# Local attention with half-summed products: additions on GpSimd and VectorE ahead of TensorE's sums, a tree for VectorE's own sums, and a last block shared anew

## The chip, the cores and the metric

One core of a Trainium2 chip runs the whole program. The metric is the device time of one execution in microseconds (us), taken over several runs. The engines are TensorE (PE), VectorE (DVE), ScalarE (ACT), GpSimd (POOL) and SyncE (SP); SBUF is the on-chip memory of 128 partitions, PSUM the memory into which TensorE accumulates.

## The reference

Four layers run one after the other on x of 8 x 512 x 256: a causal attention, a transformer layer with four experts, the local attention `_L0_attn_b_ref`, and the transformer layer once more. Each is `x = x + layer(layernorm(x))`. The change touches the local attention alone:

```python
def _L0_attn_b_ref(query, in_proj_weight, in_proj_bias, rel_pos_keys, out_w, out_b):
    t, b, e = query.shape
    scaling = D ** (-0.5)
    qkv = jnp.einsum('tbe,fe->tbf', query, in_proj_weight) + in_proj_bias
    q, k, v = jnp.split(qkv, 3, axis=-1)
    ...
    scores = jnp.einsum('btd,bsd->bts', q, k) + jnp.einsum('btd,tsd->bts', q, rel_k)
    probs = jax.nn.softmax(scores, axis=-1)
    attn = jnp.einsum('bts,bsd->btd', probs, v)
    attn = attn.transpose(1, 0, 2).reshape(t, b, e)
    return jnp.einsum('tbe,oe->tbo', attn, out_w) + out_b
```

Its first axis is the "time": x is given as it is, so there are 8 times, and 512 sequences take the place of the batch. Each of 16 heads has 16 elements. A query attends to all 8 times of its own sequence, so scores are 8 x 8 per sequence and head: far too small for matmuls over a sequence.

## The kernel before, in words

`local_attention` puts 128 sequences on the partitions and goes through four blocks (`bt`, NBT = 4). In a block, t is the time of the query and s that of the key, both 0 to 7. All is 32-bit.

For each t and block, two kinds of product of 128 x 2048 (8 keys x 256 elements) are made elementwise:
- score products, query t times all keys, which VectorE reduces over the 16 elements of a head into `s_ps` (PSUM), line 2207;
- value products, the weights of t times all values, which are then summed over the 8 keys s.

Who makes them: GpSimd makes the score products of t = 0 to 5 (`scores`, line 2362) and the value products of t = 0, 1, 2, 4, 5 (`values`, line 2370) into a ring of four buffers; VectorE makes the score products of 6 and 7 (line 2193, the query read from `a_ps` in PSUM) and the value products of 3, 6 and 7 (`own_values`, line 2243, the weights read from `s_ps` in PSUM) into `own[0]` and `own[1]`.

Who sums the value products over the keys: TensorE for t = 0 to 5 (`sum_over_keys`, line 1997), with eight matmuls by the identity that accumulate 256 columns each in one half of `att_ps`; two values of t fill it, and the next pair waits until VectorE's `normalise` (line 2263) has read it. For 6 and 7 VectorE's own reduce does it (line 2248).

Around that: TensorE projects block bt + 1 (lines 1952 to 1977) and the output of block bt - 1 (lines 2009 to 2019) while block bt's scores and weights are made, and then runs block bt's sums; in the last block there is nothing left to project ahead. ScalarE reads the projections out of PSUM and takes the exponentials (lines 2107 and 2111). VectorE adds the relative term, subtracts the maximum (`shift`), totals the weights (`total_weight`, lines 2229 and 2231), normalises and adds the residual (`add_residual`, line 2269). The order on each engine is written out by hand, and all is tied by counting semaphores, so every engine works strictly in its own written order. The transformer phases before and after are blocks of their own and don't overlap with these four.

Of the kernel before, what the change touches and what calls it, by code (L numbers as in the profile page):

```python
# [1811 lines left out]
NTM = NB  # L1812
# [9 lines left out]
N_POOL = len(POOL_QK) + len(POOL_PV)  # L1822
N_DVE = len(DVE_QK) + len(DVE_PV)
# [3 lines left out]
def local_attention(nc, ctx, C, A, x_src, x_dst):  # L1827
# [59 lines left out]
    def qk_order(t):  # L1887

        return t - DVE_QK[0] if t in DVE_QK else len(DVE_QK) + t

    def pool_item(bt, t, pv):
        return N_POOL * bt + (len(POOL_QK) + POOL_PV.index(t) if pv else POOL_QK.index(t))

    def dve_item(bt, t, pv):
        return N_DVE * bt + (len(DVE_QK) + DVE_PV.index(t) if pv else DVE_QK.index(t))

    with nc.Block() as block:
# [25 lines left out]
        def _(pe):  # L1923
# [31 lines left out]
            def project_qk(bt, t):  # L1955
# [75 lines left out]
            for bt in range(NBT):  # L2031
# [21 lines left out]
                for t in PE_SUMS:  # L2053
# [6 lines left out]
        def _(act):  # L2060
# [40 lines left out]
            def exp(bt, q):  # L2101
                act.wait_ge(shifted, 2 * bt + q + 1)
                if bt >= 1:
                    act.wait_ge(pool_prod, N_POOL * bt)
# [3 lines left out]
                first = 3 if q == 0 else 2  # L2108
# [335 lines left out]
```

## Time and profile before

| | us |
|---|---|
| median of 3 runs (2695.67 to 2700.51) | 2695.88 |
| the profiled execution | 2708.65 |
| its span, first to last instruction | 2706.9 |
| the four blocks of the local attention in it | 275.1 |
| TensorE busy over the span | 2469.7 (91%) |
| VectorE | 1834.3 (68%) |
| ScalarE | 1437.0 (53%) |
| GpSimd | 1344.7 (50%) |

These shares are means over phases with different limits. The four blocks are a tenth of the span, and what a change in them is worth is read from their own stretch: the view by windows for busy time, and the timelines of the engines for what each waits for. In a timeline a row is one instruction or several alike, merged (x32); the brackets give the idle time before it and what ended it.

### The profile page before, as it was taken

To read this page: it belongs to the slowest core of one execution; us is meant where nothing else is said; L and a number is where in the kernel's file an instruction comes from. 1 tells how busy PE (TensorE), PEld (TensorE's weight loads), DVE (VectorE), ACT (ScalarE), POOL (GpSimd) and SP (SyncE) were. 2 spreads that over 40 slices of the span, in tenths; PEclk is the share of its full clock that TensorE was granted. 3 is DMA by queue.
4 is the path that set the end of the run, shared out by engine and by line. 5 is a ranking of instruction groups with operands and counts; after the bars stand their busy time and mean duration, and the time that the engine had idled before them with its cause. 6 is when DMAs were issued, how large, how long until landed. Compare 5 with 4: busy or idle time off the path is not lost. (4 is left out here: it accounts for less than half of the span.)

```text
span 2706.9 us, 46628 instructions
## 1 busy us (share of the span) xinstructions
PE 2469.7 (91%) x15144; PEld 1428.9 (53%) x15144; DVE 1834.3 (68%) x3670; ACT 1437.0 (53%) x2991; POOL 1344.7 (50%) x1359
## 2 busy tenths in 40 slices
PE   4999999999999999989994899976999999989997
PEld 2455555554444444368894466652344444349896
DVE  3899999998778887833333566755778888844333
ACT  2666666666777777643331222102777777653332
POOL 4466555653345554246453466633335555445554
PEclk8999999999999999999997799986999999999998
DMA  5333333333434444146554000004334444335553
GB/s 149 88 107 106 99 97 106 114 114 91 120 119 130 131 125 115 48 145 195 185 194 146 0 1 16 16 31 123 107 113 129 131 130 123 91 113 176 188 200 115
DMA packets 250018, 306.35 MB, mean 113 GB/s; under 512 B 27692, under 2 KB 224945, under 8 KB 249780
## 3 DMA queue, kind: packets, MB, share of 16 engines
q1 hardware_dynamic: 239604, 277.11, 34.2%
q0 software_dynamic: 10176, 26.27, 2.7%
q8 instruction: 125, 2.05, 0.3%
q14 instruction: 113, 0.93, 0.1%
HBM read 210.85 MB, written 92.84 MB: 112 GB/s over the span
## 5 line engine op out<-in xcount | busy, mean ns | idle before, releaser
L698 DVE TENSOR_REDUCE neg_max_af<-sc_af 128x1 f32<-128x512 f32 (+3 forms) x864 | 550.8, 664 | 122.0 <-PE sc_af L414 86.2
L628 ACT ACTIVATE prob_af<-sct_af 128x512 f32<-128x512 f32 (+1 forms) x864 | 484.9, 582 | 253.7 <-PE sct_af L435 139.8
L698 DVE TENSOR_REDUCE neg_max_f<-sc_f 128x1 f32<-128x512 f32 x512 | 334.3, 685 | 102.7 <-PE sc_f L414 100.0
L628 ACT ACTIVATE prob_f<-sct_f 128x512 f32<-128x512 f32 x512 | 291.4, 598 | 143.0 <-PE sct_f L435 140.4
L414 PE MATMUL sc_af<-stack_k_af,stack_q_af 96*128 96x512 bf16 (+3 forms) x1024 | 333.0, 345 | 15.5 <-DVE neg_max_af L698 15.1
L435 PE MATMUL sct_af<-stack_q_af,stack_k_af 99*128 99x512 bf16 (+3 forms) x1024 | 331.2, 345 | 6.8 <-ACT prob_af L628 5.4
L1513 PE MATMUL hT_ps_e<-xT_e,w_r 128*128 128x128 f32 x2240 | 266.6, 278 | 5.1 <-DMA w_r<-in_f_W_dram 4.0
L1513 PEld LDWEIGHTS hT_ps_e<-xT_e,w_r 128*128 128x128 f32 x2240 | 264.4, 194 | 10.7 <-DMA w_r<-in_f_W_dram 6.0
L1500 PE MATMUL y_ps_e<-w_r,hT_e 128*128 x1120 | 256.5, 382 | 5.9 <-issue 3.8
L727 DVE SCALAR_TENSOR_TENSOR prob_af<-prob_af,w_r 128x512 f32<-128x512 f32 (+2 forms) x224 | 234.3, 1054 | 25.4 <-ACT prob_af L628 25.3
L466 PE MATMUL out_af<-prob_af,v_aug_af 128*32 128x512 f32 (+3 forms) x2048 | 231.8, 524 | 7.2 <-DVE prob_af L727 6.3
L1500 PEld LDWEIGHTS y_ps_e<-w_r,hT_e 128*128 128x128 f32 x1120 | 208.2, 191 | 35.8 <-issue 9.9
L435 PEld LDWEIGHTS sct_af<-stack_q_af,stack_k_af 99*128 99x128 bf16 x1024 | 100.0, 98 | 229.7 <-ACT prob_af L628 148.6
L1665 DVE TENSOR_TENSOR y_e<-y_ps_e,b_e 128x256 f32<-128x256 f32 x70 | 29.7, 425 | 282.3 <-PE y_ps_e L1500 278.1
L414 PE MATMUL sc_f<-stack_k_f,stack_q_f 96*128 96x512 bf16 x512 | 198.8, 390 | 9.5 <-DVE neg_max_f L698 9.5
L435 PE MATMUL sct_f<-stack_q_f,stack_k_f 99*128 99x512 bf16 x512 | 195.1, 383 | 5.9 <-ACT prob_f L628 4.4
L1550 ACT ACTIVATE xT_e<-xT_ps_e 128x256 f32<-128x256 f32 x70 | 26.9, 384 | 324.5 <-PE xT_ps_e L1491 303.5
L1561 ACT ACTIVATE hT_e<-hT_ps_e,b_r 128x128 f32<-128x128 f32 x560 | 152.8, 383 | 32.9 <-issue 26.9
L414 PEld LDWEIGHTS sc_af<-stack_k_af,stack_q_af 96*128 96x128 bf16 x1024 | 101.6, 99 | 125.3 <-DVE neg_max_af L698 61.4
L966 POOL TENSOR_TENSOR parts_af<-qkf_af,parts_af 128x512 bf16<-128x512 f32 x64 | 80.6, 1259 | 148.3 <-ACT parts_af L606 148.3
L466 PE MATMUL out_f<-prob_f,v_aug_f 128*32 128x512 f32 x1024 | 136.4, 604 | 0.8 <-ACT prob_f L628 0.7
L435 PEld LDWEIGHTS sct_f<-stack_q_f,stack_k_f 99*128 99x128 bf16 x512 | 49.6, 98 | 160.1 <-ACT prob_f L628 119.2
(358 smaller groups left out, 4658.3 us busy)
## 6 DMA issues: line engine op xcount, KB each, us to landing
w_r<-in_f_W_dram SPq DMA_DIRECT2D x78, 1024.0 KB, 6.3
k_parts_d<-parts_af SPq DMA_DIRECT2D x192, 128.0 KB
stack_k_af<-k_parts_d SPq DMA_DIRECT2D x64, 384.0 KB, 4.3
q_parts_d<-parts_af SPq DMA_DIRECT2D x96, 128.0 KB
stack_q_af<-q_parts_d SPq DMA_DIRECT2D x64, 192.0 KB, 3.0
k_parts_d<-parts_f SPq DMA_DIRECT2D x96, 128.0 KB
stack_k_f<-k_parts_d SPq DMA_DIRECT2D x32, 384.0 KB, 4.3
xt_r<-sorted_x SPq DMA_DIRECT2D x70, 128.5 KB
```

The lines of the kernel that those rows point to most:

```text
L414: last = nc.tensor.matmul(bank[:, o:o + cols], M.stack_q[0:96, g, h, qt * P:qt * P + P], M.stack_k[0:96, g, h, 0:cols], start=True, stop=True)
L435: last = nc.tensor.matmul(bank[:, o:o + T - q0], M.stack_k[0:99, g, h, kt * P:kt * P + P], M.stack_q[0:99, g, h, q0:T], start=True, stop=True)
L466: last = nc.tensor.matmul(bank[32 * i:32 * i + 32, q0:T], M.v_aug[:, kt, 4 * g + i, :], M.prob[:, kt % 2, i, 0:T - q0], start=(kt == 0), s ...
L628: nc.scalar.activation(dst, src.rearrange("p (h q) -> p h q", h=len(heads)), ACT.Exp).then_inc(S.exp_done, 1)
L698: nc.vector.tensor_reduce(M.neg_max[:, qt, heads[0]:heads[-1] + 1], src, AX.X, ALU.max, negate=True).then_inc(S.max_done, 1)
L727: nc.vector.scalar_tensor_tensor(out=p, in0=p, scalar=1.0, in1=M.floor[:, g % 2, hs, kt * P:T], op0=ALU.min, op1=ALU.max).then_inc(S.clip_ ...
L966: nc.gpsimd.tensor_tensor(M.parts[:, j, 1, :], full, top, ALU.subtract).then_inc(S.split_step, 1)
L1500: last = nc.tensor.matmul(y_ps[:, 0:D], hT[s % 2][:, c, :], w2[:, c, e, :], start=(c == 0), stop=(c == FC - 1))
L1513: last = nc.tensor.matmul(hT_ps[2 * (s % 2) + f][:, q * P:q * P + P], w1[n % NW][:, c, cols], xT[:, c, :], start=(c == 0), stop=(c == DC - 1))
L1550: nc.scalar.activation(xT[:, :, :], xT_ps[:, 0:D].rearrange("p (c t) -> p c t", c=DC), ACT.Copy).then_inc(xT_ready, 1)
L1561: last = nc.scalar.activation(hT[s % 2][:, 4 * f + q, :], hT_ps[2 * (s % 2) + f][:, q * P:q * P + P], ACT.Relu, bias=b1[:, e, 4 * f + q:4 ...
L1665: nc.vector.tensor_tensor(y[i][:, :], y_ps[:, 0:D], b2[:, e, :], ALU.add).then_inc(y_ready, 1)
```

## The change

- In blocks 0 to 2 GpSimd adds the two halves of the value products of t = 1, 2 and 5 onto each other (1024 columns), waiting for its own product first, and TensorE's sum for these takes four matmuls.
- `own_values` adds its product's halves with `fold` (1024 columns, then 512), waits between the steps, and for t = 3 leaves two slices to TensorE; for 6 and 7 a third addition of 256 columns ends in `att`. The reduce of line 2248 is gone.
- The last block is shared anew: GpSimd makes the score products of 0 to 4 and the value products of 0 to 3, VectorE the score products of 6, 7 and 5 (5 with the query from `qk` in SBUF) and the value products of 4 to 7; TensorE sums in the order 0, 1, 4, 2, 5, 3, with 4 and 5 in `b_ps` and two slices each. VectorE's order for that block is written out by itself.

```diff
-POOL_QK = (0, 1, 2, 3, 4, 5)
-DVE_QK = (6, 7)
-POOL_PV = (0, 1, 2, 4, 5)
-DVE_PV = (3, 6, 7)
-PE_SUMS = (0, 1, 2, 3, 4, 5)
+LAST = NBT - 1
+POOL_QK = [(0, 1, 2, 3, 4) if bt == LAST else (0, 1, 2, 3, 4, 5) for bt in range(NBT)]
+DVE_QK = [(6, 7, 5) if bt == LAST else (6, 7) for bt in range(NBT)]
+POOL_PV = [(0, 1, 2, 3) if bt == LAST else (0, 1, 2, 4, 5) for bt in range(NBT)]
+DVE_PV = [(4, 5, 6, 7) if bt == LAST else (3, 6, 7) for bt in range(NBT)]
+PRE_ADDED = [() if bt == LAST else (1, 2, 5) for bt in range(NBT)]
+PE_SUMS = [(0, 1, 4, 2, 5, 3) if bt == LAST else (0, 1, 2, 3, 4, 5) for bt in range(NBT)]
...
-    def qk_order(t):
-
-        return t - DVE_QK[0] if t in DVE_QK else len(DVE_QK) + t
+    def qk_order(bt, t):
+
+        order = [6, 7] + [u for u in range(8) if u < 6] if bt < LAST else [6, 0, 7, 1, 5, 2, 3, 4]
+        return order.index(t)
...
+    def summands(bt, t):
+
+        if t in PRE_ADDED[bt]:
+            return NTM // 2
+        return 2 if t in DVE_PV[bt] else NTM
+
+    def own_buf(bt, t):
+
+        if bt == LAST and t in DVE_PV[bt]:
+            return own[(4, 5, 6, 7).index(t) % 2]
+        return own[0] if t == 3 else own[1]
...
-                if t in POOL_PV:
+                if t in POOL_PV[bt]:
                     m = pool_item(bt, t, True)
                     pe.wait_ge(pool_prod, m + 1)
                     buf = ring[m % RING]
                 else:
-                    pe.wait_ge(dve_prod, dve_item(bt, t, True) + 1)
-                    buf = own[0]
+                    pe.wait_ge(own_added, added_by_vector(bt, t))
+                    buf = own_buf(bt, t)
                 n = 3 * bt + t // 2
-                if t % 2 == 0 and n >= 1:
+                sums = b_ps if bt == LAST and t >= 4 else att_ps
+                if bt == LAST and t >= 4:
+                    pe.wait_ge(b_read, NTM * NBT)
+                elif t % 2 == 0 and n >= 1:
                     pe.wait_ge(normed, 4 * ((n - 1) // 3) + (n - 1) % 3 + 1)
-                for s in range(NTM):
-                    last = nc.tensor.matmul(att_ps[:, D * (t % 2):D * (t % 2) + D], C.ident[:, :], buf[:, s * D:s * D + D],
-                                            start=(s == 0), stop=(s == NTM - 1))
+                for s in range(summands(bt, t)):
+                    last = nc.tensor.matmul(sums[:, D * (t % 2):D * (t % 2) + D], C.ident[:, :], buf[:, s * D:s * D + D],
+                                            start=(s == 0), stop=(s == summands(bt, t) - 1))
                 last.then_inc(pe_summed, 1)
...
-                first = 3 if q == 0 else 2
+                first = (3 if q == 0 else 2) if bt < LAST else (3 if q == 0 else 0)
...
+            def fold(dst, buf, cols):
+
+                folds[0] += 1
+                nc.vector.tensor_tensor(dst, buf[:, 0:cols], buf[:, cols:2 * cols], ALU.add).then_inc(fold_step, 1)
+                dve.wait_ge(fold_step, folds[0])
...
+                if t == 5:
+                    dve.wait_ge(qk_summed, NTM * bt + qk_order(bt, 7) + 1)
...
-                q = a_ps[t % 2][:, 0:D].rearrange("p (h e) -> p h e", h=H).unsqueeze(1).to_broadcast(wide)
+                q = (qk[i][:, t, 0:D] if t == 5 else a_ps[t % 2][:, 0:D]).rearrange("p (h e) -> p h e", h=H).unsqueeze(1).to_broadcast(wide)
                 nc.vector.tensor_tensor(split_heads(own[t % 2]), k, q, ALU.mult).then_inc(dve_prod, 1)
...
-                buf = own[0] if t == 3 else own[1]
+                buf = own_buf(bt, t)
                 dve.wait_ge(weights_ready, 4 * bt + (2 if t < 4 else 4))
-                if t == 3:
+                if bt < LAST and t == 3:
                     dve.wait_ge(qk_summed, NTM * bt + 2)
-                if t == 7:
+                if bt == LAST and t in (4, 5):
+                    dve.wait_ge(qk_summed, NTM * bt + NTM)
+                if bt == LAST and t in (6, 7):
+                    dve.wait_ge(pe_summed, N_SUMS * bt + PE_SUMS[bt].index(t - 2) + 1)
+                if bt < LAST and t == 7:
                     dve.wait_ge(own_summed, 2 * bt + 1)
                 v = vr[i][:, :, 0:D].rearrange("p s (h e) -> p s h e", h=H)
                 wt = s_ps[t // 4][:, (t % 4) * P:(t % 4) * P + P].rearrange("p (s h) -> p s h", s=NTM).unsqueeze(3).to_broadcast(wide)
                 nc.vector.tensor_tensor(split_heads(buf), v, wt, ALU.mult).then_inc(dve_prod, 1)
-                if t != 3:
-                    dve.wait_ge(dve_prod, dve_item(bt, t, True) + 1)
+                dve.wait_ge(dve_prod, dve_item(bt, t, True) + 1)
+                fold(buf[:, 0:4 * D], buf, 4 * D)
+                if t < 6:
+                    nc.vector.tensor_tensor(buf[:, 0:2 * D], buf[:, 0:2 * D], buf[:, 2 * D:4 * D], ALU.add).then_inc(own_added, 1)
+                else:
+                    fold(buf[:, 0:2 * D], buf, 2 * D)
                     if bt >= 1 and t == 6:
                         dve.wait_ge(oT_made, 4 * bt)
-                    nc.vector.tensor_reduce(att[:, t, :], buf[:, :].rearrange("p (s c) -> p c s", s=NTM), AX.X, ALU.add).then_inc(own_summed, 1)
+                    nc.vector.tensor_tensor(att[:, t, :], buf[:, 0:D], buf[:, D:2 * D], ALU.add).then_inc(own_summed, 1)
...
                 if j < 3:
-                    dve.wait_ge(pe_summed, len(PE_SUMS) * bt + 2 * j + 2)
+                    dve.wait_ge(pe_summed, N_SUMS * bt + max(PE_SUMS[bt].index(t) for t in (2 * j, 2 * j + 1)) + 1)
...
-                    src = att_ps[:, :].rearrange("p (t h e) -> p t h e", t=2, h=H)
+                    src = (b_ps if bt == LAST and j == 2 else att_ps)[:, :].rearrange("p (t h e) -> p t h e", t=2, h=H)
...
+            own_scores(LAST, 6)
+            pool_scores(LAST, 0)
+            own_scores(LAST, 7)
+            pool_scores(LAST, 1)
+            own_products(LAST, 5)
+            own_scores(LAST, 5)
+            add_residual(LAST - 1, 0)
+            pool_scores(LAST, 2)
+            pool_scores(LAST, 3)
+            shift(LAST, 0)
+            add_residual(LAST - 1, 1)
+            pool_scores(LAST, 4)
+            shift(LAST, 1)
+            total_weight(LAST, 0)
+            own_values(LAST, 4)
+            own_values(LAST, 5)
+            total_weight(LAST, 1)
+            normalise(LAST, 0)
+            own_values(LAST, 6)
+            normalise(LAST, 1)
+            own_values(LAST, 7)
+            normalise(LAST, 2)
+            normalise(LAST, 3)
...
-                nc.gpsimd.tensor_tensor(split_heads(ring[m % RING]), v, weight[:, t, :, :].unsqueeze(3).to_broadcast(wide),
-                                        ALU.mult).then_inc(pool_prod, 1)
+                buf = ring[m % RING]
+                made = nc.gpsimd.tensor_tensor(split_heads(buf), v, weight[:, t, :, :].unsqueeze(3).to_broadcast(wide), ALU.mult)
+                if t in PRE_ADDED[bt]:
+                    made.then_inc(pool_step, 1)
+                    pool.wait_ge(pool_step, len(PRE_ADDED[0]) * bt + PRE_ADDED[bt].index(t) + 1)
+                    made = nc.gpsimd.tensor_tensor(buf[:, 0:4 * D], buf[:, 0:4 * D], buf[:, 4 * D:8 * D], ALU.add)
+                made.then_inc(pool_prod, 1)
```

## Rows read from the trace of the kernel before

**Rows 1.** Windows view, the four blocks; per engine busy us (instructions), then PEclk, DMA.
```profile
1547.10:1607.20 60.10, 57.47 (x235) 36.90 (x234) 31.53 (x21) 16.37 (x33) 30.51 (x8) 1.00 0.00 1
1607.20:1678.80 71.60, 69.40 (x289) 44.65 (x288) 49.03 (x33) 18.05 (x36) 45.74 (x12) 1.00 0.05 15
1678.80:1750.50 71.70, 69.50 (x289) 44.67 (x288) 49.02 (x33) 14.13 (x28) 45.86 (x12) 1.00 0.05 15
1750.50:1822.20 71.70, 54.38 (x209) 38.73 (x207) 47.90 (x37) 6.38 (x12) 33.50 (x9) 0.86 0.04 15
```

**Rows 2.** Timeline of TensorE, block 1: start us, length us, engine, line, operation.
```profile
1655.78 7.07 PE L1997 MATMUL att_ps_l<-ring_l,ident 128*128 128x256 f32 x32
1663.79 3.69 PE L1997 MATMUL att_ps_l<-ring_l,ident 128*128 128x256 f32 x16 [0.93 <-DVE att_l L2263]
...
1671.86 7.14 PE L1997 MATMUL att_ps_l<-ring_l,ident 128*128 128x256 f32 x32 [0.93 <-DVE att_l L2263]
1678.84 1.04 PE L1952 MATMUL g_ps_l<-ident,xn_l 128*128 128x128 f32 x8
```

**Rows 3.** Timeline of GpSimd in the four blocks.
```profile
1572.54 14.61 POOL L2370 TENSOR_TENSOR ring_l<-vr_l,weight_l 128x2048 f32<-128x2048 f32 x4 [28.94 <-ACT weight_l L2107]
...
1644.23 14.61 POOL L2370 TENSOR_TENSOR ring_l<-vr_l,weight_l 128x2048 f32<-128x2048 f32 x4 [17.68 <-ACT weight_l L2107]
...
1663.12 9.03 POOL L2362 TENSOR_TENSOR ring_l<-qk_l 128x2048 f32<-128x2048 f32 x2
...
1769.73 18.24 POOL L2370 TENSOR_TENSOR ring_l<-vr_l,weight_l 128x2048 f32<-128x2048 f32 x5 [1.68 <-ACT weight_l L2107]
```

**Rows 4.** Timeline of VectorE, block 1.
```profile
1649.95 2.28 DVE L2243 TENSOR_TENSOR own_l<-vr_l,s_ps_l 128x2048 f32<-128x2048 f32 x1
1652.69 1.02 DVE L2229 TENSOR_REDUCE total_l<-weight_l 128x64 f32<-128x512 f32 x1 [0.47 <-ACT weight_l L2107]
...
1656.48 3.77 DVE L2248 TENSOR_REDUCE att_l<-own_l 128x256 f32<-128x2048 f32 x1
1662.95 0.69 DVE L2263 TENSOR_TENSOR att_l<-att_ps_l,inv_l 128x512 f32<-128x512 f32 x1 [2.69 <-PE att_ps_l L1997]
...
1671.03 0.69 DVE L2263 TENSOR_TENSOR att_l<-att_ps_l,inv_l 128x512 f32<-128x512 f32 x1 [1.41 <-PE att_ps_l L1997]
```

**Rows 5.** Timeline of GpSimd in the first layer.
```profile
321.20 0.74 POOL L983 TENSOR_TENSOR v_aug_af<-v_st_af,ones 128x256 f32<-128x256 f32 x1 [5.19 <-ACT v_st_af L573]
...
353.80 1.18 POOL L970 TENSOR_TENSOR parts_af<-qkf_af,parts_af 128x512 bf16<-128x512 f32 x1
355.98 1.76 POOL L983 TENSOR_TENSOR v_aug_af<-v_st_af,ones 128x256 f32<-128x256 f32 x1 [1.01 <-PE out_af L474]
357.82 1.32 POOL L990 TENSOR_TENSOR w_r<-v_aug_af 128x128 f32<-128x128 f32 x1
```

**Rows 6.** Timeline of VectorE in the same stretch.
```profile
353.99 1.02 DVE L711 TENSOR_TENSOR max_rest_af<-neg_max_af,max_parts_af 128x16 f32<-128x16 f32 x1
...
355.94 2.88 DVE L727 SCALAR_TENSOR_TENSOR prob_af<-prob_af,w_r 128x1024 f32<-128x1024 f32 x2
```

**Rows 7.** Views of single lines: count, ns min/median/max, first and last start.
```profile
L2263 DVE TENSOR_TENSOR att_l<-att_l,inv_l x4: 681/990/1002, 1608.1 to 1808.1; 128x512 f32<-128x512 f32 x4
...
L2362 POOL TENSOR_TENSOR ring_l<-qk_l x24: 4507/4532/4988, 1516.7 to 1763.5; 128x2048 f32<-128x2048 f32 x24
```

**Rows 8.** Groups by shape: count | busy us, mean ns | idle before.
```profile
L711 DVE TENSOR_TENSOR max_rest_f<-neg_max_f,max_parts_f 128x16 f32<-128x16 f32 x32 | 5.7, 179 | 1.1
...
L1602 DVE TENSOR_TENSOR x_out_r<-x_out_r,ln_b 128x1024 f32<-128x1024 f32 x2 | 2.4, 1224 | 0.1
...
L1044 POOL TENSOR_TENSOR x_out_r<-x_out_r,ln_g 128x1024 f32<-128x1024 f32 x14 | 30.6, 2186 | 0.0
```

**Rows 9.** Timeline of TensorE, block 3.
```profile
1790.05 5.84 PE L1997 MATMUL att_ps_l<-ring_l,ident 128*128 128x256 f32 x16 [7.72 <-DVE att_l L2263]
```

**Rows 10.** Windows view, 2 us at that sum's start.
```profile
1790.00:1792.00 2.00, 1.95 (x5) 1.62 (x6) 2.00 (x1) 0.00 (x0) 0.00 (x0) 0.50 0.00 0
```

More of the change, by code:

```diff
@@ L1816 @@
 NB_COLS = 3 * D + NREL * H
-POOL_QK = (0, 1, 2, 3, 4, 5)
-DVE_QK = (6, 7)
-POOL_PV = (0, 1, 2, 4, 5)
-DVE_PV = (3, 6, 7)
-PE_SUMS = (0, 1, 2, 3, 4, 5)
-N_POOL = len(POOL_QK) + len(POOL_PV)
-N_DVE = len(DVE_QK) + len(DVE_PV)
+LAST = NBT - 1
[5 more added lines that the diff above has]
+PE_SUMS = [(0, 1, 4, 2, 5, 3) if bt == LAST else (0, 1, 2, 3, 4, 5) for bt in range(NBT)]
+N_SUMS = 6
+N_POOL = [len(POOL_QK[bt]) + len(POOL_PV[bt]) for bt in range(NBT)]
+N_DVE = [len(DVE_QK[bt]) + len(DVE_PV[bt]) for bt in range(NBT)]
 RING = 4
@@ L2052, in _ @@
                         project_out(bt - 1, q)
-                for t in PE_SUMS:
+                for t in PE_SUMS[bt]:
                     sum_over_keys(bt, t)
@@ L2079, in free_inputs @@
                 if bt >= 2:
-                    act.wait_ge(pool_prod, N_POOL * (bt - 1))
-                    act.wait_ge(dve_prod, N_DVE * (bt - 1))
+                    act.wait_ge(pool_prod, sum(N_POOL[:bt - 1]))
+                    act.wait_ge(dve_prod, sum(N_DVE[:bt - 1]))
             def read_qk(bt, t):
@@ L2103, in exp @@
                 if bt >= 1:
-                    act.wait_ge(pool_prod, N_POOL * bt)
+                    act.wait_ge(pool_prod, sum(N_POOL[:bt]))
                     act.wait_ge(inv_step, 4 * bt)
@@ L2215, in shift @@
                 base = 2 * (2 * bt + q)
-                dve.wait_ge(qk_summed, NTM * bt + max(qk_order(t) for t in range(4 * q, 4 * q + 4)) + 1)
+                dve.wait_ge(qk_summed, NTM * bt + max(qk_order(bt, t) for t in range(4 * q, 4 * q + 4)) + 1)
                 dve.wait_ge(b_read, NTM * bt + NTM)
@@ L2293, in _ @@
             shift_of(1, NBT - 1)
-            for t in DVE_QK:
+            for t in (6, 7):
                 own_products(0, t)
-            for bt in range(NBT):
-                for t in DVE_QK:
+            for bt in range(NBT - 1):
+                for t in (6, 7):
                     own_scores(bt, t)
@@ L2317, in _ @@
                 normalise(bt, 1)
-                if bt + 1 < NBT:
-                    for t in DVE_QK:
-                        own_products(bt + 1, t)
+                for t in (6, 7):
+                    own_products(bt + 1, t)
                 normalise(bt, 2)
                 normalise(bt, 3)
+            own_scores(LAST, 6)
[21 more added lines that the diff above has]
+            normalise(LAST, 3)
             add_residual(NBT - 1, 0)
@@ L2349, in free_ring @@
                     return
[L2350 to L2352 removed]
+                old_bt, at = 0, m - RING
+                while at >= N_POOL[old_bt]:
+                    old_bt, at = old_bt + 1, at - N_POOL[old_bt]
+                if at < len(POOL_QK[old_bt]):
+                    pool.wait_ge(qk_summed, NTM * old_bt + qk_order(old_bt, POOL_QK[old_bt][at]) + 1)
                 else:
[L2354 removed]
+                    pool.wait_ge(pe_summed, N_SUMS * old_bt + PE_SUMS[old_bt].index(POOL_PV[old_bt][at - len(POOL_QK[old_bt])]) + 1)
             def scores(bt, t):
@@ L2375, in _ @@
             for bt in range(NBT):
-                for t in POOL_QK:
+                for t in POOL_QK[bt]:
                     scores(bt, t)
-                for t in POOL_PV:
+                for t in POOL_PV[bt]:
                     values(bt, t)
```

18 lines of the change are left out of this document (9 added, 9 removed).

## The prediction, made before the changed kernel ran

> **What bounds the kernel now.** I looked first for the stretch in which the changed function runs, with the view by windows: four blocks, 1547.1 to 1822.2 us, 275.1 of the span's 2706.9 [rows 1]. Nothing outside it is touched, and the phases on both sides are separated from it, so only these four lengths can move. In blocks 0 to 2 TensorE (PE) is busy 57.5 of 60.1, 69.4 of 71.6 and 69.5 of 71.7 us at a granted clock of 1.00: it is the bound. In block 3 it is busy 54.4 of 71.7 and the clock's mean is 0.86: there it waits for other engines.
>
> Second, TensorE's own order in block 1, which block 2 repeats to 0.02 us [rows 2]. After the next block's projections come six sums over keys; two sums take 7.07 us, so one sum of eight matmuls takes 3.54 and one matmul 0.44. Between pairs it idles only 0.93 us, for VectorE's normalisation. Third, what stands beside it. GpSimd (POOL) starts its value products at 1644.23, right behind the exponentials, and makes one every 3.65 us; a score product takes 4.52 [rows 3]. VectorE's (DVE) order behind the exponentials is product 3 (2.28 us), the weights' total with its reciprocal (1652.69 to product 6, which ends at 1656.48: 1.55), product 6 and its reduce (3.77), normalise 0 at 1662.95, product 7 and reduce, normalise 1 at 1671.03 [rows 4]. So both helpers are done just in time: normalise 0 and 1 wait for TensorE, not the other way round.
>
> **What the change removes.** In blocks 0 to 2 sums 1, 2 and 5 shrink from eight matmuls to four, sum 3 from eight to two: 18 of 48, or 18 x 0.44 = 7.9 us of TensorE per block. Two reduces of 3.77 us go too.
>
> **What it adds, uncontended.** VectorE gets eight additions: for buffer 3 two (1024 and 512 columns), for 6 and 7 three each (1024, 512, 256). A 1024-column addition takes 1.22 us [rows 8]; a 512-column product 0.68 at its shortest [rows 7]; the 256-column one I estimate at 0.42 from their difference. A tree is then 2.3 us where the reduce took 3.77, and buffer 3 costs 1.9 more. GpSimd gets three 1024-column instructions at 2.19 us [rows 8], 6.6 us per block; they stand in its queue ahead of the later products. Their waits on the instruction before cost some 0.1 us each, an estimate from GpSimd's gaps (355.98 + 1.76 to 357.82, 0.08 us) [rows 5].
>
> Laid out from 1644.23 with these alone: VectorE ends product 3 at 1652.2, its additions 1654.1, total 1655.6, product 6 at 1657.9, tree 1660.2. TensorE ends sums 0 and 1 at 1655.8 + 5.3 = 1661.1; normalise 0 to 1661.8; sums 2 and 3 to 1664.5; product 7 and tree to 1666.4, normalise 1 to 1667.0, sums 4 and 5 to 1672.4. GpSimd would have product 5 ready at 1644.2 + 18.2 + 6.8 = 1669.2, in time for that. The block would end at 1672.4, not 1678.84: 6.4 us shorter.
>
> **The term that turns it: additions with both inputs in SBUF.** Until now VectorE's large products in these blocks read one input from PSUM (the query in a_ps, the weights in s_ps), and they take 2.23 to 2.28 us whatever GpSimd does [rows 4]. All eight new additions read both inputs from SBUF. Where such instructions of VectorE meet GpSimd's, the trace shows exclusion by whole instructions, both ways:
> - A 128x16 subtraction, 0.18 us elsewhere [rows 8], starts at 353.99, 0.19 us into a GpSimd instruction that ends at 354.98, and takes 1.02: it ends at 355.01 [rows 5, 6].
> - At 355.94 two 1024-column instructions of VectorE take 2.88 us instead of 2 x 1.22. GpSimd's 355.98, whose like takes 0.74 alone, takes 1.76, so it began some 1.0 later, when the first was through; the second began when that ended [rows 5, 6]. They alternate, although VectorE's two stand back to back.
> - In this stretch: normalise 3, the only such instruction here, has a median of 0.99 us and a minimum of 0.68, and a score product has a maximum of 4.99 beside a median of 4.53 [rows 7].
> The waits end 0.13 us ahead of the recorded end of the other. I take this as the rule for the long products too. The nearest rows reach only 0.4 us into a long one, so this is the unknown; its lower bound is no wait at all (the layout above), its upper a full 3.65 or 4.52 us for each addition.
>
> The Trainium skill has the same in "SBUF — State Buffer", § Who interferes with whom: a VectorE instruction with two SBUF inputs contends with a GpSimd instruction that reads SBUF, and the shared pair of ports is held for a whole instruction while the other blocks fully. By that rule, the trace agrees (1.02 us for 0.18), the saving above is not to be had; by a sharing of bandwidth it mostly would.
>
> **Block 1 laid out again, with alternation.** GpSimd: product 0 to 1647.9, product 1 to 1651.5, its addition to 1653.8. VectorE: product 3 to 1652.2, then its 1024-addition waits to 1653.7 and ends 1654.9. GpSimd's product 2, held up, runs to 1658.4; VectorE's 512-addition waits for it, ends 1658.95. Total to 1660.5, product 6 to 1662.75. GpSimd: addition of 2 to 1661.0, product 4 to 1664.65. VectorE's tree for 6: 1664.5 to 1665.75; GpSimd's product 5 to 1669.25; VectorE 512 to 1669.75; GpSimd's addition of 5 to 1671.8; VectorE 256 to 1672.1. Normalise 0 ends 1672.75, where it ended at 1663.6. Product 7 to 1675.0; its tree waits for the next block's score products 0 and 1 (to 1676.4 and 1681.9) and ends 1682.9, the last addition free since GpSimd then waits for a ring buffer. Normalise 1 ends 1683.5, for 1671.7. TensorE, long done with sums 2 and 3, starts sum 4 at 1683.6: 5.3 us for sums 4 and 5 at full clock, end 1688.9, 10.1 later than 1678.84.
>
> The clock adds to that. TensorE now stands still for some 12 us before sum 2 and some 6 before sum 4. In block 3 of the trace it stood still 7.72 us before 1790.05, and the sum there took 5.84 us for 3.54: the granted clock was 0.50, the lower level of 1.2 GHz, when it began [rows 9, 10]. Those 2.3 us I take for sum 4; nothing and 3.5 (the whole sum at half the clock) are the bounds. The block then ends at 1691.2, **12.4 us longer**.
>
> Block 0 has the same distance from GpSimd's first value product to its end (1572.54 to 1607.2, 34.7 us, for 34.6 in block 1) [rows 1, 3] and block 2 repeats block 1, so the same for each: 3 x 12.4 = 37.2.
>
> **Block 3.** It is shared anew: GpSimd makes 5 + 4 products for 6 + 5, VectorE 3 + 4 for 2 + 3, with four trees in all, and TensorE adds 36 slices for 48 (5.3 us less). But GpSimd enters it late, with three score products left, the third waiting 2.3 us behind VectorE's product 5 (both inputs in SBUF). That product and its sum stand ahead of the residual additions, which TensorE's second output projection waits for. Laid out in the same way, an estimate with coarser steps, GpSimd has its first value product 25.5 us into the block for 19.2 [rows 3], the last ends at 40 for 37.5, and TensorE has its last sum at 58.2 for 56.9. Behind that, product 7 with its tree (4.6 us) stands between normalise 1 and the residual, while TensorE projects: the tail is 15.6 for 14.9. Sum +2; between -2 (TensorE's saving gets through at the clock's upper level) and +6.
>
> **Sum.** 37.2 + 2 = 39.2 us. The profiled execution would take 2708.65 + 39 = 2748; it lies 12.8 above the median of the timed runs, so the median goes from 2695.88 to **2735 us**. Low: 3 x 10.1 - 1.5 = 28.8, so 2725; high: 3 x 15 + 5 = 50, so 2746. With a little for the phases of the alternation, 2721 to 2751.
>
> **The rivals.**
> 1. *No wait, or a short one, behind long products* (the other side). The port is held only for a part of a 3.65 or 4.52 us instruction, so VectorE's additions slip in. For it: the only rows in a long product reach 0.4 us into its end. Against it: a 1.18 us GpSimd instruction held VectorE for all that was left. Price: 3 x -6.4 - 1.4 = -20.6, so 2675; with 0.3 us per addition and 0.45 per 512 columns on GpSimd [rows 7] some 2.3 per block remain: 2689. It decides where the median wait of a 1024-addition is under some 0.8 us. Chance 0.09.
> 2. *The tree goes through as a group.* VectorE keeps the port for all three additions, so each tree waits once. Then tree 6 ends at 1663.4, tree 7 at 1669.1, and GpSimd's last addition at 1674.9 sets the end: 1676.7, 2.1 shorter. 3 x -2.1 + 1 = -5.3: 2691. Against it: 2.88 and the 1.76 between. Chance 0.06.
> 3. *The forecast without the clock's fall*: 3 x 10.1 + 2 = 32: 2728. It is inside the range.
> That the change doesn't shorten TensorE's sums is excluded: it issues fewer matmuls of the same shape.
>
> **Chances.** Forecast with rival 3: 0.85; rivals 1 and 2: 0.09 and 0.06. The range holds nearly all of the first, some 0.81. A difference of 0.2% (5.4 us) is about what timing this kernel can tell from none. Faster by more: 0.09 and half of rival 2, 0.12; within: 0.03; slower: 0.85.
>
> **What would show it.** In the profile after: VectorE's 1024- and 512-column additions in the local attention with medians of 2.5 to 4.5 us and not 1.22 and 0.68, with the shortest ones near the latter, in block 3 after GpSimd's last product; VectorE's products with a PSUM input still at 2.26; GpSimd's products over 3.65 by up to 1.1 where an addition went ahead; TensorE idle some 12 us before sum 2 in the name of VectorE's normalise, and some 6 before sum 4; blocks of 73, 84, 84 and 74 us. Additions of 1.2 to 1.6 us beside a busy GpSimd would make the prediction wrong, and blocks of 54, 65 and 65 us would be their result. If the additions wait but normalise 0 isn't late, the layout is wrong. If sum 4 takes 3.5 us, the clock term is.

## The result, and the profile after

The changed kernel takes 2742.28 us (median of 4 runs, 2736.83 to 2745.46) where the kernel before takes 2696.74 (4 runs, 2695.67 to 2700.51): ratio 1.0164, 95% interval 1.0142 to 1.0186. It is slower by 45.5 us; 2735 was forecast, with 2721 to 2751 as the range.

In what follows, product t, sum t and tree t are those of the query time t (a tree is VectorE's chain of additions of 1024, 512 and 256 columns for t = 6 or 7), and normalise j is the instruction for t = 2j and 2j + 1.

Time first, by the four blocks. The view by windows of the profile after (per engine, PE, PEld, DVE, ACT, POOL: busy us and instructions; then the granted clock), to be read against [rows 1]:

```profile
1535.70:1609.30 73.60, 54.14 (x199) 33.23 (x197) 48.22 (x27) 16.37 (x33) 40.01 (x12) 0.86 0.00 0
1609.30:1694.60 85.30, 66.27 (x254) 41.09 (x253) 67.39 (x39) 18.05 (x36) 56.54 (x15) 0.88 0.04 13
1694.60:1779.90 85.30, 66.31 (x253) 41.08 (x252) 67.41 (x39) 14.12 (x28) 56.50 (x15) 0.88 0.04 13
1779.90:1853.50 73.60, 47.46 (x185) 32.82 (x183) 58.21 (x47) 6.60 (x12) 28.14 (x7) 0.81 0.04 15
```

The last block ends at 1854.05, so the four take 318.3 us for 275.1, 43.2 more. TensorE issues 36 records fewer in block 0 and is busy 3.3 us less, and yet the first three blocks are each 13.5 to 13.7 us longer: it waits, and the mean granted clock falls from 1.00 to 0.86 and 0.88. The profiled execution took 2739.55 us, only 30.9 more than the one of before; the parts outside the blocks, which the change doesn't touch, were 12.3 us shorter in it. So the block lengths are compared here, not the spans.

TensorE in block 1 (timeline: start, length, line; in brackets the idle time before and what ended it), against [rows 2]:

```profile
1657.90 5.35 PE L2021 MATMUL att_ps_l<-ring_l,ident 128*128 128x256 f32 x24
1675.53 3.55 PE L2021 MATMUL att_ps_l<-ring_l,ident 128*128 128x256 f32 x8 [12.28 <-DVE att_l L2305]
1678.92 1.03 PE L2021 MATMUL att_ps_l<-own_l,ident 128*128 128x256 f32 x4
1686.35 8.40 PE L2021 MATMUL att_ps_l<-ring_l,ident 128*128 128x256 f32 x24 [6.41 <-DVE att_l L2305]
1694.60 1.04 PE L1973 MATMUL g_ps_l<-ident,xn_l 128*128 128x128 f32 x8
```

The two idle times were 0.93 each in [rows 2]; they are 12.28 and 6.41, both ended by VectorE's normalisation (line 2305). The x24 of the first pair of sums takes 5.35 us and the x24 of the last pair 8.40, which is the clock; the window at its start:

```profile
1686.00:1688.00 2.00, 1.65 (x4) 1.41 (x5) 2.00 (x2) 0.00 (x0) 0.00 (x0) 0.50 0.04 8
```

GpSimd in block 1, against [rows 3] (line 2437 makes the value products, 2441 is the new addition, 2428 makes the next block's score products):

```profile
1646.35 7.32 POOL L2437 TENSOR_TENSOR ring_l<-vr_l,weight_l 128x2048 f32<-128x2048 f32 x2 [17.68 <-ACT weight_l L2131]
1653.75 2.35 POOL L2441 TENSOR_TENSOR ring_l<-ring_l 128x1024 f32<-128x1024 f32 x1
1656.06 4.67 POOL L2437 TENSOR_TENSOR ring_l<-vr_l,weight_l 128x2048 f32<-128x2048 f32 x1
1660.80 2.70 POOL L2441 TENSOR_TENSOR ring_l<-ring_l 128x1024 f32<-128x1024 f32 x1
1663.47 8.29 POOL L2437 TENSOR_TENSOR ring_l<-vr_l,weight_l 128x2048 f32<-128x2048 f32 x2
...
1674.46 10.13 POOL L2428 TENSOR_TENSOR ring_l<-qk_l 128x2048 f32<-128x2048 f32 x2
```

VectorE beside it, against [rows 4] (2281 product, 2213 and 2285 additions, 2290 the last of a tree):

```profile
1652.08 2.28 DVE L2281 TENSOR_TENSOR own_l<-vr_l,s_ps_l 128x2048 f32<-128x2048 f32 x1
1654.39 2.79 DVE L2213 TENSOR_TENSOR own_l<-own_l 128x1024 f32<-128x1024 f32 x1
1657.22 4.06 DVE L2285 TENSOR_TENSOR own_l<-own_l 128x512 f32<-128x512 f32 x1
...
1662.73 2.23 DVE L2281 TENSOR_TENSOR own_l<-vr_l,s_ps_l 128x2048 f32<-128x2048 f32 x1
1664.99 7.31 DVE L2213 TENSOR_TENSOR own_l<-own_l 128x1024 f32<-128x1024 f32 x2
1672.34 2.45 DVE L2290 TENSOR_TENSOR att_l<-own_l 128x256 f32<-128x256 f32 x1
1674.71 0.68 DVE L2305 TENSOR_TENSOR att_l<-att_ps_l,inv_l 128x512 f32<-128x512 f32 x1
...
1677.61 7.54 DVE L2213 TENSOR_TENSOR own_l<-own_l 128x1024 f32<-128x1024 f32 x2
1685.18 0.43 DVE L2290 TENSOR_TENSOR att_l<-own_l 128x256 f32<-128x256 f32 x1
```

Read the two lists together. VectorE's addition of 1654.39 ends at 1657.18, 1.1 us after GpSimd's addition (to 1656.10); GpSimd's product of 1656.06 takes 4.67 for 3.65, since it stood behind VectorE's; the 512-column addition waits that product out and ends at 1661.28, GpSimd's addition of 1660.80 takes 2.70 for 2.35. Here they alternate. Tree 6 is 9.8 us long (1664.99 to 1674.79) where the reduce took 3.77, and normalise 0 stands behind it; tree 7 meets the score products in the same way. The products of line 2281, with the weights in PSUM, are at 2.23 and 2.28 as before.

In block 3, once GpSimd has made its last product, the same instructions on VectorE:

```profile
1823.96 1.23 DVE L2213 TENSOR_TENSOR own_l<-own_l 128x1024 f32<-128x1024 f32 x1
1825.22 0.69 DVE L2285 TENSOR_TENSOR own_l<-own_l 128x512 f32<-128x512 f32 x1
...
1830.18 1.95 DVE L2213 TENSOR_TENSOR own_l<-own_l 128x1024 f32<-128x1024 f32 x2
1832.17 0.43 DVE L2290 TENSOR_TENSOR att_l<-own_l 128x256 f32<-128x256 f32 x1
```

1.23, 0.69 and 0.43 us, a tree in 2.4. Over the four blocks, by shape (count, busy us, mean ns, idle before):

```profile
L2213 DVE TENSOR_TENSOR own_l<-own_l 128x1024 f32<-128x1024 f32 x13 | 30.9, 2376 | 0.4
...
L2213 DVE TENSOR_TENSOR own_l<-own_l 128x512 f32<-128x512 f32 x8 | 28.1, 3516 | 0.3
```

A 512-column addition costs more than a 1024-column one: the length is the wait, not the work.

### The profile page after: what moved, and what is told of

It reads as the page before. It is cut to its first block and busy times, and to the rows that moved or that the text cites. A ratio compares the mean times of both kernels' runs of the same rounds, so it can differ in the third digit from the quotient of the medians.

```text
span 2737.8 us, 46402 instructions
## 1 busy us (share of the span) xinstructions
PE 2447.1 (89%) x15012; PEld 1409.5 (51%) x15012; DVE 1895.7 (69%) x3698; ACT 1436.7 (52%) x2991; POOL 1367.5 (50%) x1366
## 5 line engine op out<-in xcount | busy, mean ns | idle before, releaser
L635 ACT ACTIVATE w_r<-sct_af,minus 128x512 f32<-128x512 f32 x128 | 87.6, 687 | 86.5 <-PE sct_af L449 85.1
```

The costliest lines, as they stand in the source:

```text
L635: nc.scalar.activation(M.floor[:, g % 2, i, :], M.sct[u % 2][:, :], ACT.Exp, bias=C.minus100[:, 0:1]).then_inc(S.exp_done, 1)
```

## The experiments

Theory: VectorE's additions with both inputs in SBUF and GpSimd's instructions exclude each other as wholes, and that wait, on the way to normalise 0 and 1, with the clock's fall behind it, is the whole loss in blocks 0 to 2. Rival: the loss is work that was put on the helpers (three GpSimd additions per block, two instructions for one reduce) or the new last block. Three kernels do one part alone and a fourth two of them; they come from one source with three switches. The lengths of the blocks of all kernels are in a table at the end of this section. (The ratios and intervals are those of the recorded comparisons with the kernel before; the quotients of the two medians differ from them by up to 0.0013.)

```diff
+LASTNEW, VTREE, PADD = False, False, True
-LAST = NBT - 1
+LAST = NBT - 1 if LASTNEW else NBT
-PRE_ADDED = [() if bt == LAST else (1, 2, 5) for bt in range(NBT)]
+PRE_ADDED = [() if bt == NBT - 1 or not PADD else (1, 2, 5) for bt in range(NBT)]
+TREE = [VTREE and bt < NBT - 1 or bt == LAST for bt in range(NBT)]
...
+                if not TREE[bt]:
+                    if t != 3:
...
+                        nc.vector.tensor_reduce(att[:, t, :], buf[:, :].rearrange("p (s c) -> p c s", s=NTM), AX.X, ALU.add).then_inc(own_summed, 1)
+                    return
```

**GpSimd's additions alone** (PADD).

> Part of the change alone: GpSimd's additions for t = 1, 2, 5 in blocks 0 to 2; VectorE keeps its reduces, sum 3 keeps eight slices, the last block is as before. Exclusion by whole instructions (the forecast's theory): VectorE has no new instruction with two SBUF inputs here, so nothing of GpSimd's is held up; TensorE saves 12 of 48 matmuls, 5.3 us, of which some 4.9 shorten each block: 55, 67, 67 us, the last within 2 of 71.7; in all 13 to 15 us faster than the kernel before, 2682 us; GpSimd's additions 2.2 to 2.4 us each. Rival A (it is GpSimd's additions ahead of its later products that made the blocks longer): blocks as long as before or longer, 2696 or more. Rival B (VectorE simply has too much work in the changed kernel): says nothing against a gain here.

2695.39 us for 2703.3 (0.9984, 0.9965 to 1.0003): in device time it can't be told from the kernel before, where 2682 was expected. The profile shows more: the blocks are 264.2 us, 10.9 shorter than before. Blocks 0 to 2 give 5.0 us each, nearly all of the 12 matmuls that TensorE saves (12 x 0.44 = 5.3). So the work put on GpSimd costs nothing there by itself: that rival falls. The last block, whose code is that of before, is 4.0 us longer. Normalise 3, with both inputs in SBUF, is the place (the line's view: count, ns min/median/max; then VectorE and GpSimd at the third of them):

```profile
L2318 DVE TENSOR_TENSOR att_l<-att_l,inv_l x4: 681/4556/4601, 1591.7 to 1785.9; 128x512 f32<-128x512 f32 x4
```

```profile
1725.11 4.55 DVE L2318 TENSOR_TENSOR att_l<-att_l,inv_l 128x512 f32<-128x512 f32 x1
```

```profile
1720.10 27.37 POOL L2443 TENSOR_TENSOR ring_l<-qk_l 128x2048 f32<-128x2048 f32 x6
```

It starts beside the second of GpSimd's six products, which now follow each other without a gap, and takes 4.55 us for 0.68. In blocks 1 and 2 this is hidden behind TensorE's projections. In block 3 the residual behind it is 3.5 us late, and so is TensorE's second projection (12.7 us into the block for 9.2).

**VectorE's trees alone** (VTREE, blocks 0 to 2).

> Part of the change alone: VectorE's additions for t = 3, 6, 7 in blocks 0 to 2, sum 3 with two slices; GpSimd adds nothing, the last block is as before. Exclusion by whole instructions: the additions wait for products of 3.65 and 4.52 us, blocks of 67, 79, 79 us, in all 20 us slower than before, 2716; TensorE saves 2.7 us per block and that shows nowhere. Rival A (GpSimd's additions are the cause): 57 to 59, 69, 69, so some 8 us faster, 2688. Rival B (VectorE's load: eight additions of 1.22, 0.68 and 0.42 us for two reduces of 3.77, in all 0.9 us less): no change or faster.

2726.77 us (1.0097, 1.0063 to 1.0132); the blocks 297.6, 22.5 longer: 7.9, 7.4 and 7.1 in blocks 0 to 2, though GpSimd has no more work than before and TensorE 6 matmuls less. The trees are the loss. In block 1 it lies before and in sum 2:

```profile
1673.14 6.06 PE L2027 MATMUL att_ps_l<-ring_l,ident 128*128 128x256 f32 x16 [8.52 <-DVE att_l L2318]
```

TensorE idles 8.52 us for normalise 0, where it idled 0.93, and the sum takes 6.06 for 3.69: 10.0 us, of which the 6 matmuls give 2.6 back. The rest of the changed kernel's 13.6 per block comes only where both parts meet: together they are some 6.2 worse than the trees alone, where the GpSimd additions alone are 5.0 better. Tree 7 shows why (VectorE, GpSimd and TensorE in block 1):

```profile
1675.22 1.95 DVE L2219 TENSOR_TENSOR own_l<-own_l 128x1024 f32<-128x1024 f32 x2
1677.21 0.43 DVE L2303 TENSOR_TENSOR att_l<-own_l 128x256 f32<-128x256 f32 x1
```

```profile
1679.28 4.54 POOL L2443 TENSOR_TENSOR ring_l<-qk_l 128x2048 f32<-128x2048 f32 x1 [9.16 <-PE att_ps_l L2027]
```

```profile
1680.99 7.14 PE L2027 MATMUL att_ps_l<-ring_l,ident 128*128 128x256 f32 x32 [0.93 <-DVE att_l L2318]
```

Here GpSimd has run out of ring buffers and stands still for 9.16 us while VectorE makes tree 7, in 2.4 us; TensorE idles 0.93 before sum 4 and runs it at the upper level of the clock (7.14, as in [rows 2]). In the changed kernel the three additions keep GpSimd behind, it is still at the score products during tree 7, and the second wait of 6.4 us, and the slow sums behind it, are there.

**The new last block alone** (LASTNEW).

> Part of the change alone: the last block shared anew, blocks 0 to 2 as before. By the layout with exclusion the block's length stays within 2 us of 71.7: TensorE's 5.3 us less and GpSimd's two products less are paid back by VectorE's score product 5 ahead of the residual and by the product and tree behind normalise 1: 2696, within 3 us of before. Rival C (the last block is the part that pays, the first three the part that costs): 5 us or more faster.

2701.22 us (0.9998, 0.9981 to 1.0014); its last block is 73.2 us for 71.7, the others are those of before. The last block loses 1.5 us in the profile, which the timed runs can't show.

**GpSimd's additions and the new last block** (PADD and LASTNEW).

> GpSimd's additions in blocks 0 to 2 and the last block shared anew, without VectorE's trees in blocks 0 to 2. The trees that remain are those of the last block, which end after GpSimd's last product. Exclusion by whole instructions: blocks of 55, 67, 67 us as with GpSimd's additions alone; the last one is longer than the 74 of the changed kernel, 75 to 80 us, since it is entered earlier against GpSimd's queue and product 5 of VectorE (two SBUF inputs, 2048 columns) and normalise 3 each wait for a score product of 4.52 us. In all 6 to 9 us faster than the kernel before. Rival: GpSimd's two products less let the last block gain: under 71.

2693.75 us (0.9978, 0.9958 to 0.9999). Blocks 1 and 2 are at 66.7, the last at 76.0, as long as with the old last block (75.7). Normalise 3 took 4.57 us again; VectorE's product 5, which was expected to wait for GpSimd too, took 2.29 and did not; GpSimd's five score products of that block took 24.93 for 5 x 4.53 = 22.7, so it was GpSimd that waited. (Block 0 took 57.7 for 55.1, since TensorE entered it at the lower level of its clock.) So the new order of the last block doesn't take back what normalise 3's wait costs.

**The same instructions with a PSUM input.** The changed kernel, with the second input of each VectorE addition taken from `s_ps`, so that the same shapes run in the same places with the same waits between them. The halves themselves are left unsummed in it.

```diff
+            def add_psum(dst, buf, cols, t):
+                ps = s_ps[t // 4]
+                if cols <= 2 * D:
+                    return nc.vector.tensor_tensor(dst, buf[:, 0:cols], ps[:, 0:cols], ALU.add)
...
-                nc.vector.tensor_tensor(dst, buf[:, 0:cols], buf[:, cols:2 * cols], ALU.add).then_inc(fold_step, 1)
+                add_psum(dst, buf, cols, t).then_inc(fold_step, 1)
```

> The changed kernel with every addition of VectorE reading its second input from PSUM (columns of s_ps) in place of the buffer's other half: same count, same shapes, same waits, same order on all engines; what it adds is not the halves' sum, so the attention's values are not the reference's. Exclusion by whole instructions between instructions that read two SBUF inputs: additions of 1.22, 0.68 and 0.42 us, blocks of 55, 66, 66 and 68 us, 18 to 20 us faster than the kernel before: 2677 and 65 below the changed kernel. Rivals A and B (GpSimd's additions, VectorE's load, the added waits of VectorE on itself): all of these are unchanged, so 2740 as the changed kernel.

2687.66 us (0.9936, 0.9917 to 0.9956; the changed kernel stands at 1.0164); blocks 56.3, 65.4, 67.0 and 73.6. The views of the lines, 13 additions each of 1024 and 512 columns, and the 8 that end a tree:

```profile
L2215 DVE TENSOR_TENSOR own_l<-own_l,s_ps_l x13: 1220/1221/1223, 1580.9 to 1796.1; 128x1024 f32<-128x1024 f32 x13
```

```profile
L2214 DVE TENSOR_TENSOR own_l<-own_l,s_ps_l x13: 686/686/689, 1582.2 to 1797.4; 128x512 f32<-128x512 f32 x13
L2214 DVE TENSOR_TENSOR att_l<-own_l,s_ps_l x8: 420/420/422, 1588.5 to 1798.1; 128x256 f32<-128x256 f32 x8
```

Not one of them waited, beside a GpSimd that makes the same products, and GpSimd's value products are back at a mean of 3.68 (4.05 in the changed kernel). The one thing changed in the instructions is which second input they read, and so where it lies. That settles the cause in blocks 0 to 2. The Trainium skill states this side of the rule too ("SBUF — State Buffer", § Who interferes with whom: an instruction of VectorE with at most one SBUF input doesn't contend with GpSimd); these rows agree. Block 3 stays at 73.6, where 68 was expected: nearly all of its loss comes with its new order (73.2 with the last block alone), not with the additions' waits.

**The wait measured by itself.** The kernel before, with additions of two columns on VectorE behind value product 3: one in block 0, three in a row in block 1, and three in block 2 with one input in PSUM.

```diff
+            def probe(bt):
+                for k in range((0, 1, 4)[bt], (1, 4, 7)[bt]) if bt < 3 else ():
+                    second = s_ps[0][:, 0:2] if bt == 2 else half[:, 16:18]
+                    nc.vector.tensor_tensor(scratch[:, 2 * k:2 * k + 2], half[:, 0:2], second, ALU.add)
```

> The disputed wait by itself: the kernel before, with additions of 128x2 on VectorE right behind product 3, while GpSimd runs its value products of 3.65 us back to back. Block 0: one such addition with both inputs in SBUF; block 1: three of them back to back with no wait between them; block 2: three with the second input in PSUM. Exclusion by whole instructions with alternation: the one in block 0 takes 2.0 to 3.5 us (what is left of the product that runs), those in block 1 the same and then some 3.6 us each, 9 to 11 us in all, those in block 2 0.06 to 0.2 us each. Rival 1 of the prediction (the port is held for a part only): under 1 us each. Rival 2 (VectorE's go through as a group): 2 to 3.5 us for all three. Block 1 becomes some 6 to 8 us longer by the first, unchanged by the others.

2708.4 us in one run, for 2699.47 of the kernel before. The view of the line, then VectorE in block 0 and in block 1:

```profile
L2254 DVE TENSOR_TENSOR scratch_l<-half_l x4: 148/3058/3649, 1576.3 to 1651.1; 128x2 f32<-128x2 f32 x4
L2254 DVE TENSOR_TENSOR scratch_l<-half_l,s_ps_l x3: 149/149/150, 1724.6 to 1724.7; 128x2 f32<-128x2 f32 x3
```

```profile
1576.35 3.06 DVE L2254 TENSOR_TENSOR scratch_l<-half_l 128x2 f32<-128x2 f32 x1
...
1648.03 6.70 DVE L2254 TENSOR_TENSOR scratch_l<-half_l 128x2 f32<-128x2 f32 x3
```

An addition of two columns that starts early in a product of 3.65 us takes 3.06, and 0.149 with an input in PSUM. The wait exists in the long products, from near their start, and for two columns as well as for 1024. That is the row the trace of before didn't have, and it excludes rival 1. The rule of the Trainium skill that the prediction weighed ("SBUF — State Buffer", the same section: the shared pair is held for a whole instruction) agrees with the 3.06 us. In one thing I was wrong: three in a row should have taken 9 to 11 us if they alternated strictly. They took 6.70, and the block 4.9 us more (76.5) where 6 to 8 were expected. The first waited out a product, one took 0.148, so it got in right behind the first, and the third, which began at 1651.1, waited 3.65, a whole product. So alternation is how the longer, dependent additions meet GpSimd, not a rule for each pair; whether their length or their dependence makes the difference was not tested.

**The gap filled.** The changed kernel, with nine matmuls into `b_ps` (free at that time) ahead of sum 4, in the time in which TensorE waits for normalise 1. They end before it does, and only the clock can change.

```diff
+                if bt < LAST and t == 4:
+                    pe.wait_ge(b_read, NTM * (bt + 2))
+                    for _ in range(9):
+                        nc.tensor.matmul(b_ps[:, 0:D], C.ident[:, :], w_o[:, 0, :], start=True, stop=True)
```

> The changed kernel with nine more matmuls of TensorE (identity times a weight, into b_ps, read by nobody) ahead of sum 4 in blocks 0 to 2, in the 6.4 us in which it waits for normalise 1. Nothing else changes. The clock's term: sums 4 and 5 take 5.4 to 6 us instead of 8.4, the granted clock is back at 1.00 before they begin, each block is 2.5 to 3 us shorter, 8 in all (blocks 71, 82.5, 82.5): 0.3% less than the changed kernel. If the clock isn't the cause of the 8.4 us: no change, or longer where the nine reach over the end of the wait.

Blocks 0 to 2 are 72.3, 82.3 and 82.3 us, 1.3, 3.0 and 3.0 shorter than in the changed kernel; 71 was expected for block 0. TensorE's sums 4 and 5 in block 0, the filling and these sums in block 1, and the windows view of the latter:

```profile
1602.18 7.13 PE L2025 MATMUL att_ps_l<-ring_l,ident 128*128 128x256 f32 x24 [1.91 <-DVE att_l L2309]
...
1680.63 4.28 PE L2018 MATMUL b_ps_l<-w_o_l,ident 128*128 128x256 f32 x18
1686.12 5.45 PE L2025 MATMUL att_ps_l<-ring_l,ident 128*128 128x256 f32 x24 [1.21 <-DVE att_l L2309]
```

```profile
1686.10:1691.40 5.30, 5.28 (x24) 4.62 (x25) 4.36 (x2) 0.00 (x0) 1.48 (x1) 1.00 0.00 0
```

In block 1 the same 24 records take 5.45 us at a granted clock of 1.00, and 8.40 without the filling. The start of the sums is the same in both, 77.0 us into the block. So the clock term is real and is 3.0 us in blocks 1 and 2. In block 0 the same filling helped less: it ended 1.91 us before the sums and not 1.21, the granted clock was 0.50 in the middle of them, and they took 7.13. The PSUM-input kernel shows the same two outcomes after equal idle times, in block 1 and block 2:

```profile
1663.00 5.42 PE L2021 MATMUL att_ps_l<-ring_l,ident 128*128 128x256 f32 x24 [2.40 <-DVE att_l L2313]
...
1728.36 7.11 PE L2021 MATMUL att_ps_l<-ring_l,ident 128*128 128x256 f32 x24 [2.40 <-DVE att_l L2313]
```

So the idle time just before a sum doesn't alone tell what the clock will cost it. The whole kernel, 2737.7 us (1.0149, 1.0113 to 1.0185), can't be told from the changed one.

**The part that pays, without its wait.** GpSimd's additions as in the first kernel, and VectorE's two reduces write into `b_ps`, so that normalise 3 has one input in PSUM. TensorE waits for normalise 3 before it writes `b_ps` for a later block, and the wait that protects `att` moves from the reduce to normalise 3.

```diff
-                        nc.vector.tensor_reduce(att[:, t, :], buf[:, :].rearrange("p (s c) -> p c s", s=NTM), AX.X, ALU.add).then_inc(own_summed, 1)
+                        nc.vector.tensor_reduce(b_ps[:, D * (t - 6):D * (t - 6) + D], buf[:, :].rearrange("p (s c) -> p c s", s=NTM), AX.X, ALU.add).then_inc(own_summed, 1)
...
-                    src = a
+                    src = b_ps[:, :].rearrange("p (t h e) -> p t h e", t=2, h=H)
```

> A version meant to be faster than both: GpSimd's additions for t = 1, 2, 5 in blocks 0 to 2, VectorE's reduces for 6 and 7 as before but written to b_ps in PSUM, so that normalise 3 has one input in PSUM; all else is the kernel before. Normalise 3 took 4.55 us in the last block with GpSimd's additions alone, where it takes 0.68 by itself. Exclusion between instructions with two SBUF inputs: normalise 3 0.7 us in every block, blocks of 55, 66.6, 66.7 and 72 us, 14 to 15 us less than the kernel before (0.5%), 2682 against its 2696. Rival (the last block's 4 us are not normalise 3's wait but GpSimd's late scores): the last block stays at 75 to 76, 11 us less in all.

2684.61 us (0.9946, 0.9929 to 0.9963), faster than both kernels. Normalise 3 and TensorE's sum 2 in the last block:

```profile
L2322 DVE TENSOR_TENSOR att_l<-b_ps_l,inv_l x4: 679/680/680, 1594.4 to 1780.9; 128x512 f32<-128x512 f32 x4
```

```profile
1764.99 3.69 PE L2029 MATMUL att_ps_l<-ring_l,ident 128*128 128x256 f32 x16 [2.87 <-DVE att_l L2322]
```

0.68 in all four places, where the median was 4.56. Blocks 0 to 2 keep their 5.0 us, and the last is 68.0 (72 was expected), 7.7 shorter than with GpSimd's additions alone and 3.7 shorter than before. Of the 7.7, 5.5 is normalise 0, which ends earlier in the block (37.9 us into it for 43.4), 3.9 of it by normalise 3 itself; the other 2.2 are the clock, with sum 2 at 3.69 us for 5.88. Of the 3.7, 1.5 is normalise 0 (37.9 for 39.4), and 2.2 is the clock again: TensorE idles 2.87 us before sum 2 and takes 3.69 for it, where it idled 7.72 and took 5.84 [rows 9]. No run changes the clock at this sum by itself, so it is not shown that this part would come back in another kernel.

The block lengths, in us:

| kernel | block 0 | 1 | 2 | 3 | sum |
|---|---|---|---|---|---|
| before | 60.1 | 71.6 | 71.7 | 71.7 | 275.1 |
| changed | 73.6 | 85.3 | 85.3 | 74.1 | 318.3 |
| GpSimd's additions alone | 55.1 | 66.7 | 66.7 | 75.7 | 264.2 |
| trees alone | 67.9 | 79.0 | 78.8 | 71.9 | 297.6 |
| last block alone | 60.1 | 71.6 | 71.7 | 73.2 | 276.6 |
| additions and last block | 57.7 | 66.7 | 66.7 | 76.0 | 267.1 |
| PSUM inputs | 56.3 | 65.4 | 67.0 | 73.6 | 262.3 |
| gap filled | 72.3 | 82.3 | 82.3 | 75.1 | 312.0 |
| additions, normalise 3 from PSUM | 55.1 | 66.7 | 66.7 | 68.0 | 256.5 |

## Why the prediction was right, step by step

- **The cause.** Taken from two short meetings in the first layer [rows 5, 6], it holds in the long products: the PSUM-input kernel and the two-column addition show it. It was the step with the widest bounds, and everything else hung on it.
- **The layout of the waits.** Measured from the start of block 1, forecast and then found: VectorE's first addition ends at 47.7 and 47.9; GpSimd's product 2, held up, at 51.2 and 51.4; normalise 0 at 65.6 and 66.1; normalise 1 at 76.3 and 76.9; sum 4 starts at 76.4 and 77.05. TensorE's idle times were 12.28 and 6.41 for "some 12" and "some 6". The 0.6 us is mostly GpSimd's addition, 2.35 for the 2.19 of [rows 8].
- **The clock** was mis-sized: 2.3 us taken from [rows 9], 2.95 by the filled gap (8.40 to 5.45). The upper bound, 3.5, held it.
- **The block**: 12.4 us longer by the forecast, 13.5 to 13.7 found; in block 1, 0.65 of the difference is the later start of sum 4 and 0.65 the clock (8.25 us from that start to the next block for 7.6). The block's loss adds up from the rows: 16.8 us more idle time (12.28 and 6.41 for twice 0.93) and 4.6 of clock (1.6 at sum 2, where the engine would else have been idle, and 3.0 at sums 4 and 5), less the 7.9 of the 18 matmuls, make 13.5. Blocks of 72.5, 84.0, 84.1 and 73.7 follow from the forecast, 73.6, 85.3, 85.3 and 74.1 were found.
- **Block 3**: +2 forecast, +2.4 found. GpSimd's first value product started 25.6 us into it (25.5 forecast), its last ended at 41.3 (40), the last sum at 58.3 (58.2), the tail was 15.8 (15.6). The last block alone is +1.5. One step of this coarse layout did not happen, though: GpSimd's third score product did not wait 2.3 us behind VectorE's product 5. The three took 14.05 us together (3 x 4.53 = 13.6), and product 5 began only as the last of them ended (2.44 us long). What made up for it is not shown, so the close agreement here is in part luck.
- **The sum**: 39.2 forecast, 43.2 found in the profiles, 45.5 in the medians. The 2.3 between these two are within what the runs scatter. The step from profile to median was luck: the profiled execution was to take 2748, 12.8 above the median as before, and took 2739.55, 2.7 below it, since its parts outside the blocks were 12.3 shorter.
- **Rival 1** (no wait in long products) would have given blocks of 54, 65 and 65 us. The PSUM-input kernel comes near that case, at 56.3, 65.4 and 67.0: the uncontended layout was right to 0.4 us in block 1, its wait of 2.5 us before sum 4 included (2.40 found), and short by 2 in the other two, where the mean clock was 0.95 and 0.97. **Rival 2** (the tree goes as a group) falls by tree 6 at 9.8 us. **Rival 3** (no fall of the clock) is the filled gap: 3.0 us of a block go with it in blocks 1 and 2, 1.3 in block 0. The clock's first fall, at sum 2 (3.55 us for the 8 records, 1.97 in the last kernel), doesn't lengthen the block, since sum 4 waits for VectorE anyway.
- **What the prediction had not seen.** Normalise 3 was named as the only instruction of its kind in this stretch [rows 7], and not priced: it goes from 0.99 to 2.71 us in the changed kernel and to 4.56 with GpSimd's additions alone. And the parts were laid out only together. One at a time, GpSimd's additions are a gain of 5.0 us in each of the first three blocks, hidden in a change that loses 13.6; the forecast could not have said that the better half was worth keeping.

## What to carry to other kernels

Before work is moved to VectorE beside a busy GpSimd, look at where its inputs lie: in these runs it waited, with both in SBUF, for the GpSimd instruction under way to end, however little it did (3.06 us for two columns, 9.8 for a tree of three), and with one in PSUM it did not. Splitting one instruction into a dependent chain multiplies such waits, so count the instructions that can meet GpSimd and price each at what is left of GpSimd's instruction at that time, up to a whole one. And a change of several parts is laid out part by part as well as whole: here one half was a gain, and moving one result to PSUM freed it.

## What the runs showed of the hardware

- A two-column addition of VectorE with both inputs in SBUF took 3.06 us beside a GpSimd instruction of 3.65, and the third of three in a row took 3.65, while the second took 0.148.
- With one input in PSUM, 34 additions in the same blocks, most of them beside a working GpSimd, took what they take alone: 1.22, 0.69 and 0.42 us for 1024, 512 and 256 columns.
- GpSimd pays as well, though less: its value products of 3.65 took up to 4.73, behind a VectorE addition that takes 1.22 alone, and its additions 2.70 for 2.35, behind one of 0.69.
- After 6.4 us of idle time TensorE's 24 records of sums took 8.40 us, with a granted clock of 0.50 in the first 2 us; after 1.2 us of it, with the gap filled, 5.45 at 1.00. After 2.40 us in the PSUM-input kernel they took 5.42 in one block and 7.11 in the next.
